# Decoder kernel on one core: attention outputs packed and divided by way of DMAs instead of transposes, scores in 64x64 array tiles, last keys in 32x32 tiles

## The chip, the cores and the metric

The kernel runs on one core of a Trainium2 chip. The metric is the device time of one execution in microseconds (us). Five engines work side by side and meet only at semaphores: PE (TensorE, matrix products into the eight PSUM banks), DVE (VectorE), ACT (ScalarE), POOL (GpSimd) and SP (SyncE, which here only issues DMAs). Each engine takes its instructions strictly in the order of the program.

## What is computed

Two decoder layers over x (4 batches, 512 positions, 128 features), float32, each sublayer followed by a residual sum and a layer norm:

```python
# layer 0: causal self attention, 16 heads of 8
scores = einsum('bshd,bthd->bhst', layernorm(q) / sqrt(8), layernorm(k)); softmax, causal
out = einsum('bhst,bthd->bshd', attn, v) @ W_out
# layer 0: cross attention, 16 heads of 8, 154 keys of the context
# layer 0: mixture of 8 experts (gates under 0.1 dropped)
# layer 1: linear attention (elu + 1), causal
# layer 1: cross attention, 8 heads of 128, 154 keys
# layer 1: gated feed-forward layer, 128 -> 384 -> 128
```

The change concerns the first two lines' attentions. A head has only 8 features, so neither the scores nor the weighted values fill the 128x128 array.

## The kernel before, in words

**Turns.** Self (a = 0) and cross (a = 1) attention of a batch b go by groups g of four heads: 32 turns (b, a, g), in the order of TURNS. The remaining sublayers of a batch ("rests", lines with x2T, gate, ex, lkq, XS, PT, XO, hid, down) are cut into small steps and laid between the turns. One list of steps, `schedule()`, is the program of all engines: every engine walks the whole list and issues what it has for each step. The order of that list is written out by hand as the string MERGE, the PSUM bank of each step as the digits of BANK_OF. Within the order an engine waits only for semaphores, and PE waits until a bank that it fills has been drained.

**A turn.** `scores` (S, L1117) computes scores with queries on partitions, for the maxima alone. Each "unit" fills a pair of banks, one for the upper 64 partitions of the packed queries and keys (r = 0), one for the lower (r = 1). A self unit is one or two pieces of causal length, and then four products with an identity that add the mask of the diagonal blocks (L1136). DVE takes the maxima from PSUM (`maxima`, L1832, L1837). `max_T` (mT, L1201) turns them into rows, ACT copies these, and SP places them by one DMA (L804) among the query rows, which `scores_T` (ST, L1158, mask L1165, last keys L1149) waits for: it computes the same scores with keys on partitions, the maxima already taken off. ACT writes their exponentials to EX (L1570). `values` (PV) multiplies with V (self, L1192) or with VX (cross, L1179), whose ninth column is 1, so each head yields 8 weighted values and the sum of its weights in its own 32 partitions. The 26 keys beyond 128 of the cross attention are one full product over all four heads, L1182, through the matrix VXR.

**From a turn to the output.** ACT copies the bank to `pvraw` (L1474). `products_T` (cT, L1204) transposes it in four pieces so that heads lie along the free axis, and DVE divides (`divided`, a reciprocal L1858 and a product L1860 into ctx). After the fourth turn `ctx_T` (L1209) transposes the four blocks of ctx back to features on partitions, ACT copies them to ctxT, and `out_product` (L1213, products L1220) multiplies with the output weights. The steps ctxT, out and norm of (b, a) are called a finish below; there are eight.

**Placements.** Queries and keys of a batch are split in three bf16 parts, and SP places them by 12 DMAs for self (L783) and 12 for cross attention (L797).

## Time and profile before

| | us |
|---|---|
| three runs | 486.65, 489.23, 489.41 (median 489.23) |
| the profiled execution, its time | 487.79 |
| its span from first to last instruction | 486.0 |
| PE busy | 459.1 (94%) |
| weight loads of PE busy | 304.6 (63%) |
| DVE busy | 378.0 (78%) |
| ACT busy | 344.3 (71%) |
| POOL busy | 187.5 (39%) |

The profiled execution took 1.8 us more than its span and lies 1.4 us below the median. A matrix product is pipelined: its recorded length has a tail that overlaps the next one, so what a group of products costs is read as the distance from its start to the start of the next group, not as its length. Products and weight loads of float32 are recorded twice each, transposes once.

### The profile page before, as it was taken

To read this page: it belongs to the slowest core of one execution; us is meant where nothing else is said; L and a number is where in the kernel's file an instruction comes from. 1 tells how busy PE (TensorE), PEld (TensorE's weight loads), DVE (VectorE), ACT (ScalarE), POOL (GpSimd) and SP (SyncE) were. 2 spreads that over 40 slices of the span, in tenths; PEclk is the share of its full clock that TensorE was granted. 3 is DMA by queue.
4 is the path that set the end of the run, shared out by engine and by line. 5 is a ranking of instruction groups with operands and counts; after the bars stand their busy time and mean duration, and the time that the engine had idled before them with its cause. 6 is when DMAs were issued, how large, how long until landed. Compare 5 with 4: busy or idle time off the path is not lost.

```text
span 486.0 us, 11581 instructions
## 1 busy us (share of the span) xinstructions
PE 459.1 (94%) x4048; PEld 304.6 (63%) x4048; DVE 378.0 (78%) x1083; ACT 344.3 (71%) x879; POOL 187.5 (39%) x349
## 2 busy tenths in 40 slices
PE   6687899999999999999999999999999999999995
PEld 4454557655455556666777565567764756896895
DVE  4489888798898999995798888847878678765557
ACT  3535758877868788877757787985776868958742
POOL 8590002650204452533233331433414536835423
PEclk9589999999999999999999999999999999999999
DMA  7851300033210211200003000030000000000001
GB/s 229 189 131 36 100 5 25 13 100 82 58 24 1 67 39 35 69 2 0 4 16 93 9 3 2 3 81 13 3 12 14 0 1 2 1 1 1 2 1 43
DMA packets 27181, 18.34 MB, mean 38 GB/s; under 512 B 8217, under 2 KB 26773, under 8 KB 26997
## 3 DMA queue, kind: packets, MB, share of 16 engines
q1 hardware_dynamic: 23413, 15.44, 12.0%
q10 hardware_dynamic: 3712, 2.17, 1.8%
q8 instruction: 33, 0.54, 0.5%
q14 instruction: 23, 0.19, 0.1%
HBM read 5.58 MB, written 1.05 MB: 14 GB/s over the span
## 4 chain that ended last, share of the span: by engine, by line
PE 38%; POOL 5%; DVE 4%; ACT 3%; issue 3%; SPq 1%; DMA 1%; POOLq 0%; DVEq 0%; ACTq 0%
PE psum L1066 5%; PE psum L1425 4%; PE psum L1436 4%; PE psum L1402 3%; PE psum L1338 3%; PE psum L1129 2%; PE psum L1158 2%; PE psum L1192 2%; PE psum L1182 2%; PE psum L1179 2%; SPq L797 1%; PE psum L1447 1%; POOL GP L1024 1%; POOL rstd_rest L955 1%; ACT REST L1653 1%
## 5 line engine op out<-in xcount | busy, mean ns | idle before, releaser
L1570 ACT ACTIVATE EX<-psum 128x1024 f32<-128x1024 f32 (+1 forms) x128 | 118.1, 979 | 12.9 <-PE psum L1165 8.3
L1837 DVE TENSOR_REDUCE mparts<-psum 128x2 f32<-128x768 f32 (+1 forms) x96 | 77.5, 861 | 4.8 <-PE psum L1136 4.5
L1832 DVE TENSOR_REDUCE mparts<-psum 128x4 f32<-128x616 f32 (+1 forms) x80 | 67.8, 875 | 4.7 <-PE psum L1129 4.0
L1129 PE MATMUL psum<-K,Q 64*128 64x154 bf16 (+4 forms) x512 | 47.4, 268 | 5.6 <-issue 2.1
L1024 POOL TENSOR_TENSOR GP<-REST,xrs 128x512 f32<-128x512 f32 (+1 forms) x48 | 33.1, 713 | 46.6 <-DVE xrs L2066 32.6
L1158 PE MATMUL psum<-Q,K 64*128 64x512 bf16 (+3 forms) x320 | 41.4, 315 | 3.6 <-DMA Q<-mrows 1.8
L1653 ACT ACTIVATE REST<-psum,nxmax 128x154 f32<-128x154 f32 x96 | 36.2, 396 | 10.1 <-DVE nxmax L2056 7.9
L1474 ACT COPY pvraw<-psum 128x512 f32<-128x512 f32 x32 | 18.7, 584 | 32.4 <-PE psum L1192 23.4
L1192 PE MATMUL psum<-EX,V 128*32 128x256 f32 (+3 forms) x512 | 37.7, 435 | 0.0
L1129 PEld LDWEIGHTS psum<-K,Q 64*128 64x128 bf16 x512 | 19.0, 95 | 28.9 <-issue 18.4
L952 POOL TENSOR_SCALAR rstd_rest<-moments_rest 128x2 f32<-128x2 f32 x32 | 7.3, 228 | 74.9 <-DVE moments_rest L1872 74.4
L952 POOL TENSOR_SCALAR rstd_attn<-moments_attn 128x4 f32<-128x4 f32 x8 | 1.9, 238 | 83.9 <-DVE moments_attn L1872 83.8
L2056 DVE TENSOR_REDUCE nxmax<-psum 128x2 f32<-128x308 f32 x64 | 28.8, 469 | 5.6 <-PE psum L1402 5.2
L1402 PE MATMUL psum<-GP,xT 128*128 128x308 f32 x96 | 30.5, 433 | 0.1
L1192 PEld LDWEIGHTS psum<-EX,V 128*32 128x32 f32 x512 | 14.6, 109 | 18.4 <-issue 16.9
L1136 PE MATMUL psum<-maskS,ident 64*128 64x128 bf16 (+2 forms) x320 | 24.7, 232 | 0.0
L1698 ACT ACTIVATE X<-Y_rest,shift_rest,rstd_rest 128x128 f32<-128x128 f32 x36 | 15.9, 493 | 11.8 <-POOL shift_rest L960 11.7
L1425 PE MATMUL psum<-VM,REST 128*128 128x128 f32 x192 | 23.8, 277 | 0.2 <-DVE VX L1928 0.2
L955 POOL TENSOR_TENSOR rstd_rest<-rstd_rest,power 128x2 f32<-128x2 f32 x32 | 22.9, 716 | 2.7
L1165 PE MATMUL psum<-maskT,ident 64*128 64x128 bf16 (+2 forms) x320 | 23.8, 227 | 0.0
L1425 PEld LDWEIGHTS psum<-VM,REST 128*128 128x128 f32 x192 | 22.6, 192 | 1.3 <-issue 0.7
L1158 PEld LDWEIGHTS psum<-Q,K 64*128 64x128 bf16 x320 | 13.0, 94 | 15.9 <-issue 6.8
(343 smaller groups left out, 1150.2 us busy)
## 6 DMA issues: line engine op xcount, KB each, us to landing
Q<-xparts SPq DMA_DIRECT2D x24, 128.0 KB
Q<-parts SPq DMA_DIRECT2D x21, 128.0 KB
K<-parts SPq DMA_DIRECT2D x21, 128.0 KB
X<-in_x SPq DMA_DIRECT2D x4, 256.0 KB, 3.1
Q<-in_L_xattn_Wkv SPq DMA_DIRECT2D x1, 1024.0 KB, 7.2
K<-xkparts SPq DMA_DIRECT2D x24, 38.5 KB
out<-XB_rest SPq DMA_DIRECT2D x6, 128.0 KB, 1.8
Q<-in_L_xattn_Wq SPq DMA_DIRECT2D x1, 512.0 KB, 4.3
```

What stands on the lines that cost most here:

```text
L955: return nc.gpsimd.tensor_tensor(to, to, half_power, ALU.pow)
L1024: last = nc.gpsimd.tensor_tensor(of.XP[:, at:at + 4 * n].rearrange("p (h c) -> p h c", h=4)[:, :, 0:c1 - c0], of.XE[:, :, c0:c1], of.xrs.r ...
L1129: last = mm(to[:, r, at:at + n], Q6[a][p, b % 2, 2 * g + jj, P * q:P * q + P], K6[a][p, b % 2, 2 * g + jj, 0:n], start=at == 0 or bool(a), ...
L1158: last = mm(to[:, r, at:at + n], K6[a][p, b % 2, 2 * g + jj, P * k:P * k + P], Q6[a][p, b % 2, 2 * g + jj, P * k:S], start=at == 0 or bool ...
L1192: last = mm(to[32 * h:32 * h + 32, P * k:S], V[:, k, 4 * g + h, :], EX[:, ex_slot(b, a, g, u) + h % 2, at:at + n], start=k == PV_ORDER[0], ...
L1402: fills_(mm(fill(key)[:, 0:2 * C], half_of(b, h).xT[4][:, P * q:P * q + P], G[:, head:head + 2, :].rearrange("p h c -> p (h c)")), key)
L1425: mm(to, of.XPT[:, head, :], VM[:, head, :], start=head == 0, stop=False)
L1570: drains(nc.scalar.activation(dst, src, ACT.Exp), key)
L1653: last = nc.scalar.activation(of.XE[:, i, :], src[:, C * j:C * j + C], ACT.Exp, bias=of.nxmax[:, i:i + 1], accum_out=of.xsum[:, i:i + 1])
L1832: last = vec.tensor_reduce(nmax[:, :, :, q], src[:, :, 0:2 * n].rearrange("p r (j k) -> p r j k", j=2), AX.X, ALU.max, negate=True)
L1837: last = vec.tensor_reduce(nmax[:, :, jj, q], src[:, :, at:at + P * (q + 1)], AX.X, ALU.max, negate=True)
L2056: vec.tensor_reduce(of.nxmax[:, 2 * side:2 * side + 2], src, AX.X, ALU.max, negate=True).then_inc(xmax_ready[z], 1)
```

## The change

1. The weights of the values are laid out so that the 8 weighted values of a head fall on partitions 0, 4, ..., 28 of its 32 and the sum on partition 1. After ACT's copy to pvraw, two DMAs on SP's queue (`pack`) put the values of the turn on 32 neighbouring partitions of `weighed[a]` and the four rows of sums, cut in eighths, on 32 partitions of `sums_of[a]`. The four transposes of `products_T` and DVE's two operations per turn are gone.
2. Once per finish DVE inverts the sums in place (128x64, `invert`), one DMA writes them to DRAM (`keep_inverses`), another reads them back with each head's row repeated on 8 partitions into ctxT (`spread_inverses`, step "fan"), and DVE multiplies (`divide`, 128x512). The transposes of `ctx_T` and ACT's copy are gone.
3. Scores: where a product had 64 rows and 128 columns of the array, there are now two of 64x64 (`in_tiles`), four tiles in all. In self attention each half of the queries or keys takes only its causal length; the masks go by the same tiles.
4. Cross values: a pair of banks holds the two halves of the queries. The last keys are eight products of 32x32 tiles with 256 columns (`rests`), in place of one 128x128 product of 512 columns; the scores of these keys are laid out to match.
5. MERGE and BANK_OF are written anew for the new steps. A memset of POOL is cut in eight.

```diff
 def finish_steps(b, a):
+    yield b, "invert", a
+    yield b, "fan", a
     yield b, "ctxT", a
     yield b, "out", a
     yield b, "norm", a
...
+            def pack(b, a, g):
+
+                drained(sp, (b, "PV", a, g))
+                if b or g:
+                    sp.wait_ge(packed[a], 32 * (NQ * b + g))
+                if b and g == 0:
+                    sp.wait_ge(divided[a], b)
+                at = slice(32 * g, 32 * g + 32)
+                sp.dma_start(sums_of[a][at, :], pvraw[1:P:32, :]).then_inc(packed[a], 16)
+                sp.dma_start(weighed[a][at, :], pvraw[0:P:4, :]).then_inc(packed[a], 16)
+
+            def keep_inverses(b, a):
+
+                i = finishes.index((b, a))
+                sp.wait_ge(inverted, i + 1)
+                if i:
+                    sp.wait_ge(inverses_spread, 16 * i)
+                sp.dma_start(inverses.rearrange("h (c t) -> (h c) t", c=HD), sums_of[a][:, :]
+                             ).then_inc(inverses_kept, 16)
+
+            def spread_inverses(b, a):
+
+                i = finishes.index((b, a))
+                sp.wait_ge(inverses_kept, 16 * (i + 1))
+                if i:
+                    b0, a0 = finishes[i - 1]
+                    filled(sp, (b0, "out", a0))
+                sp.dma_start(ctxT[:, :], inverses.rearrange("h (o t) -> h o t", o=1).to_broadcast(
+                    [H, HD, S])).then_inc(inverses_spread, 16)
...
+            def in_tiles():
+
+                for e in R:
+                    for r in R:
+                        yield e, r, *[slice(TILE * i, TILE * i + TILE) for i in (e, r)]
...
                 for at, jj, q in PIECES[a][u]:
-                    n = C if a else P * (q + 1)
-                    for r in R:
-                        p = slice(TILE * r, TILE * r + TILE)
-                        last = mm(to[:, r, at:at + n], Q6[a][p, b % 2, 2 * g + jj, P * q:P * q + P],
-                                  K6[a][p, b % 2, 2 * g + jj, 0:n], start=at == 0 or bool(a), stop=bool(a))
+                    for e, r, half, p in in_tiles():
+
+                        n = C if a else P * q + TILE * (e + 1)
+                        last = mm(to[half, r, at:at + n],
+                                  Q6[a][p, b % 2, 2 * g + jj, P * q + TILE * e:P * q + TILE * e + TILE],
+                                  K6[a][p, b % 2, 2 * g + jj, 0:n], start=bool(a) or at == 0,
+                                  stop=bool(a), skip_group_check=not a)
...
+                    to = pair(key)
+                    for n in HALVES:
+                        for h in range(4):
+                            mm(to[32 * h:32 * h + 32, n, 0:HS], VX[:, 4 * g + h, :],
+                               EX[:, ex_slot(b, a, g, h // 2) + h % 2, HS * n:HS * n + HS],
+                               start=True, stop=False, skip_group_check=True)
+                    for n, h, rest, cols in rests():
+                        last = mm(to[32 * h:32 * h + 32, n, 0:HS], VXR[rest, 4 * g + h, :],
+                                  EX[rest, ex_slot(b, a, g, 2), cols], start=False, stop=True,
+                                  skip_group_check=True)
...
-            def products_T(b, a, g):
-                drained(pe, (b, "PV", a, g))
-                transposes((b, "cT", a, g), [(P * n, pvraw[:, P * n:P * n + P])
-                                             for n in range(NB)])
-
-            def ctx_T(b, a):
-                drained(pe, (b, "cT", a, NQ - 1))
-                to_features((b, "ctxT", a), ctx[a][:, :, :, :].rearrange("p n h d -> p n (h d)"))
-
             def out_product(b, a):
-                drained(pe, (b, "ctxT", a))
+                pe.wait_ge(divided[a], b + 1)
...
+            def products_out(b, a, g):
+                key = (b, "PV", a, g)
+                filled(act, key)
+                if TURN[b, a, g]:
+
+                    b0, a0, g0 = TURNS[TURN[b, a, g] - 1]
+                    act.wait_ge(packed[a0], 32 * (NQ * b0 + g0 + 1))
...
+            def invert(b, a):
+
+                dve.wait_ge(packed[a], 32 * NQ * (b + 1))
+                vec.reciprocal(sums_of[a][:, :], sums_of[a][:, :]).then_inc(inverted, 1)
+
+            def divide(b, a):
+
+                dve.wait_ge(inverses_spread, 16 * (finishes.index((b, a)) + 1))
+                vec.tensor_tensor(ctxT[:, :], weighed[a][:, :], ctxT[:, :], ALU.mult
+                                  ).then_inc(divided[a], 1)
```

One line of the table of the order, before and now (the last turn and finish of batch 3 lie near its end):

```diff
-    "1101pp0p00kf1kkf101100k10fk0112k2122310032310031022210023001100113321100321110113200"
+    "pptttk11p0pxp1pf01k11f1k0010kkfkkf1011001f100112312230213102002130223100311002013010"
```

**Place 1: PE, two units of self scores.** Before: a unit of keys times queries for two pieces of one head pair (384 and 128 columns) with its masks, and the start of one with a single piece of 512.

```order
L1129 MATMUL psum<-K_0,Q_0 128x384 x2
L1129 MATMUL psum<-K_0,Q_0 128x128 x2
L1136 MATMUL psum<-maskS,ident 128x2x64 x2
L1136 MATMUL psum<-maskS,ident 128x256 x2
L1158 MATMUL psum<-Q_0,K_0 128x512 x2
L1165 MATMUL psum<-maskT,ident 128x64 x2
L1165 MATMUL psum<-maskT,ident 128x128 x2
```

Now, the same kinds of unit (the two stand in another stretch):

```order
L1217 MATMUL psum<-Q_0,K_0 64x512 x2
L1217 MATMUL psum<-Q_0,K_0 64x448 x2
L1172 MATMUL psum<-maskT,ident 64x64 x2
L1172 MATMUL psum<-maskT,ident 64x128 x2
...
L1190 MATMUL psum<-K_0,Q_0 64x320 x2
L1190 MATMUL psum<-K_0,Q_0 64x384 x2
L1190 MATMUL psum<-K_0,Q_0 64x64 x2
L1190 MATMUL psum<-K_0,Q_0 64x128 x2
L1172 MATMUL psum<-maskS,ident 64x256 x2
L1172 MATMUL psum<-maskS,ident 64x2x64 x2
```

A unit with one piece went from 6 to 8 products, one with two pieces from 8 to 12; each product writes 64 partitions instead of 128.

**Place 2: PE, the finish of batch 3's self attention** (L1220 before and L1279 now are its output product; K_1 and Q_1 belong to cross attention). Before:

```order
L1129 MATMUL psum<-K_1,Q_1 128x154 x8
L1066 MATMUL psum<-ident,ctx_self 128x128 x4
L1353 MATMUL psum<-lwv,xT 128x128 x2
L1129 MATMUL psum<-K_1,Q_1 128x154 x8
L1179 MATMUL psum<-EX,VX 32x512 x4
L1182 MATMUL psum<-EX,VXR 128x512
L1220 MATMUL psum<-wout,ctxT 128x128 x4
```

Now:

```order
L1190 MATMUL psum<-K_1,Q_1 64x154 x8
L1111 MATMUL psum<-ident,X 128x128 x2
L1217 MATMUL psum<-Q_1,K_1 64x512 x8
L1244 MATMUL psum<-EX,VX 32x256 x8
L1248 MATMUL psum<-EX,VXR 32x256 x8
L1269 MATMUL psum<-identb,mparts 80x128
L1111 MATMUL psum<-ident,REST 128x128 x2
L1461 MATMUL psum<-GP,xT 128x308
L1190 MATMUL psum<-K_1,Q_1 64x154 x8
L1279 MATMUL psum<-wout,ctxT 128x128 x4
```

The transposes of ctx are gone, the last keys are eight small products, and a cross unit has 8 score products (a row of x8 was two units before and is one now). From the last self values of batch 3 to this output product the list has 34 steps, where it had 22.

**Place 3: DVE, the last finish** (batch 3, cross attention; what waits for packed1 and inverses_spread waits for DMAs). Before:

```order
L1872 BN_AGGR moments_rest<-stats_rest 128x2
L1858 RECIPROCAL rsum<-psum 128x16 [waits bank_filled0,bank_drained0]
L1860 TENSOR_TENSOR ctx_cross<-psum,rsum 128x4x32 [waits dve_step]
L2005 TENSOR_TENSOR vaug<-psum,rows 128x2x128 [waits bank_filled3]
L1998 TENSOR_TENSOR REST<-REST 128x512 [waits phi_exps0]
L1883 TENSOR_TENSOR Y_attn<-psum,XB_attn 128x512 [waits residual_ready,x_ready2,bank_filled1]
```

Now:

```order
L2031 TENSOR_TENSOR gl<-gl,gs 128x16 [waits dve_step]
L1924 RECIPROCAL sums_cross<-sums_cross 128x64 [waits packed1]
L2039 TENSOR_TENSOR Y_rest<-psum,X 128x256 [waits rest_x_ready1,bank_filled2]
L2053 SCALAR_TENSOR_TENSOR Y_rest<-psum,gl,Y_rest 128x128 [waits bank_filled0,bank_drained2,gates_ready1]
...
L2063 TENSOR_TENSOR REST<-REST 128x512 [waits phi_exps0]
L1929 TENSOR_TENSOR ctxT<-weighed_cross,ctxT 128x512 [waits inverses_spread]
L1950 TENSOR_TENSOR Y_attn<-psum,XB_attn 128x512 [waits residual_ready,x_ready2,bank_filled7]
```

The reciprocal moved from behind a PSUM bank to behind two DMAs, with the expert sums (L2053) queued behind it, and the product that makes ctxT stands behind two DMAs more.

## Rows read from the trace of the kernel before

**Rows 1.** Page: busy time, and three rows of the 40 slices.
```profile
PE 459.1 (94%) x4048; PEld 304.6 (63%) x4048; DVE 378.0 (78%) x1083; ACT 344.3 (71%) x879; POOL 187.5 (39%) x349
...
PE   6687899999999999999999999999999999999995
...
DVE  4489888798898999995798888847878678765557
```
**Rows 2.** Busy us by stretch; then PEclk, DMA share, GB/s.
```profile
27.00:391.00 364.00, 354.99 (x3424) 222.59 (x3425) 303.99 (x807) 270.85 (x618) 123.54 (x227) 1.00 0.13 33
391.00:486.00 95.00, 87.93 (x575) 71.03 (x573) 61.78 (x225) 62.90 (x242) 44.91 (x86) 0.99 0.02 7
90.00:210.00 120.00, 117.85 (x1185) 67.25 (x1184) 108.70 (x292) 94.09 (x189) 45.90 (x74) 1.00 0.19 49
```
**Rows 3.** Timeline of PE from 228 us: start, length, engine, line.
```profile
228.78 0.60 PE L1066 MATMUL psum<-ident,pvraw 128*128 128x128 f32 x4
229.21 0.22 PE L1201 MATMUL psum<-identb,mparts 128*80 128x128 bf16 x1
```
**Rows 4.** Timeline of PE from 222 us: the values of a cross turn.
```profile
222.30 1.07 PE L1179 MATMUL psum<-EX,VX 128*32 128x512 f32 x8
223.30 1.12 PE L1182 MATMUL psum<-EX,VXR 128*128 128x512 f32 x2
224.26 0.93 PE L1066 MATMUL psum<-ident,GP 128*128 128x128 f32 x7
```
**Rows 5.** Timeline of PE from 64 us: self units following each other.
```profile
64.24 0.39 PE L1129 MATMUL psum<-K,Q 64*128 64x384 bf16 x4
...
64.63 0.38 PE L1158 MATMUL psum<-Q,K 64*128 64x512 bf16 x2
64.85 0.25 PE L1165 MATMUL psum<-maskT,ident 64*128 64x64 bf16 x4
64.93 0.38 PE L1129 MATMUL psum<-K,Q 64*128 64x384 bf16 x4
```
**Rows 6.** Timeline of PE from 319 us: scores of the last keys.
```profile
319.58 0.40 PE L1149 MATMUL psum<-Q,K 64*32 64x512 bf16 x4
319.96 1.27 PE L1402 MATMUL psum<-GP,xT 128*128 128x308 f32 x4
```
**Rows 7.** Timeline of all engines at 310 us: two cross units.
```profile
310.02 0.44 PE L1129 MATMUL psum<-K,Q 64*128 64x154 bf16 x8
...
310.39 0.77 PE L1066 MATMUL psum<-ident,GP 128*128 128x128 f32 x5
```
**Rows 8.** Weight loads by form: busy us, mean ns | idle us before.
```profile
L1129 PEld LDWEIGHTS psum<-K,Q 64*128 64x128 bf16 x512 | 19.0, 95 | 28.9 <-issue 18.4 <-ACT EX L1570 2.9 <-DMA Q<-xparts 1.7
...
L1201 PEld LDWEIGHTS psum<-identb,mparts 128*80 128x80 bf16 x32 | 3.7, 117 | 2.4 <-issue 2.0
```
**Rows 9.** DVE by form, same columns.
```profile
L1858 DVE RECIPROCAL rsum<-psum 128x16 f32<-128x16 f32 x32 | 8.0, 249 | 3.8 <-PE psum L1066 3.6
...
L1860 DVE TENSOR_TENSOR ctx_self<-psum,rsum 128x128 f32<-128x128 f32 x16 | 4.7, 292 | 0.5
...
L1998 DVE TENSOR_TENSOR REST<-REST 128x512 f32<-128x512 f32 x6 | 4.2, 697 | 2.4 <-ACT REST L1640 2.4
```
**Rows 10.** Longest of SP's own waits: total us, times, longest.
```profile
SPq L445 <- ACT mrows L1579: 199.6, 30, 13.9
```
**Rows 11.** The DMA of the maxima: ns min/median/max; who waited for it, us, times.
```profile
L804 SPq DMA_DIRECT2D Q<-mrows x32: 707/765/852, 35.9 to 369.2; - x32
...
  PE psum L1158: 1.8, 2
```
**Rows 12.** Chain of waits: the flight of the last DMA of a placement.
```profile
326.68 2.46 DMA Q<-xparts
```
**Rows 13.** Timeline of all engines at the last finish.
```profile
380.50 0.58 ACT L1474 COPY pvraw<-psum 128x512 f32<-128x512 f32 x1 [0.87 <-PE psum L1182]
...
384.44 1.16 PE L1220 MATMUL psum<-xwo,ctxT 128*128 128x128 f32 x8
```

More of the change, by code:

```diff
@@ L257, in takes @@
         return [(b, "PV", *at)]
-    if what == "cT":
-        return [(b, "PV_out", *at)]
+    if what == "pack":
+        return [(b, "PV_out", *at)] + ([(b - 1, "ctxT", at[0])] if b else [])
+    if what == "invert":
+        return [(b, "pack", at[0], NQ - 1)]
+    if what == "fan":
+        return [(b, "invert", at[0])]
     if what == "ctxT":
-        return [(b, "cT", at[0], NQ - 1)]
+        return [(b, "fan", at[0])]
     if what == "out":
@@ L328, in in_pair @@
 def in_pair(step):
-    return step[1] in ("S", "ST") and not (step[1] == "ST" and step[2] and step[4] == 2)
+    _, what, *at = step
+    return (what == "S" or what == "ST" and not (at[0] and at[2] == 2)
+            or what == "PV" and at[0] == 1)
 STREAMS = "stpfrlwcvxu0123k"
 MERGE = (
-    "rrrrrrrrlwrrlllwrrrurrsssssuuuvuuuuussssstttrsrttslssspptssttttpsslsrppsttststtupllu"
-    "sssppststtsttpuussssppttpsufswttfuusstsusssfwpptursxffttsurrrrrctstspcfccppttpstsrrw"
-    "kttkssrpspllttssttptssssslppsstpsskfsttftsstppstsflwsppssptsktsrtssfpfctppsstcstpssp"
@@ L495, in build @@
         causal = sb("causal", [P, P], BF16)
[L497 removed]
+        ident2 = sb("ident2", [P, TILE], BF16)
         maskS = sb("maskS", [P, 2, P], BF16)
@@ L1004, in wM @@
                     pool.wait_ge(bank_filled[k], m + 1)
-                    nc.gpsimd.memset(words(Q6[1].rearrange("p b h t -> p (b h) t")), 0.0
-                                     ).then_inc(cross_rows_ready, 1)
+                    zeroed = words(Q6[1].rearrange("p b h t -> p (b h) t"))
+                    for i in range(8):
+                        last = nc.gpsimd.memset(zeroed[:, S * i:S * i + S], 0.0)
+                    last.then_inc(cross_rows_ready, 1)
                     step(nc.gpsimd.memset(XP, 0.0))
@@ L1125, in scores @@
                 for at, jj, q in PIECES[a][u]:
[L1126 to L1138 removed]
+                    for e, r, half, p in in_tiles():
+                        n = C if a else P * q + TILE * (e + 1)
[3 more added lines that the diff above has]
+                                  stop=bool(a), skip_group_check=not a)
+                if not a:
+                    last = mask(to, [at + P * q for at, _, q in PIECES[0][u]], maskS,
+                                [slice(0, P), slice(TILE, P)])
                 fills_(last, key)
@@ L1579, in max_T @@
                 drains(copy(mrows[:, parity(b, a, g), :], src[0:48, 0:64].bitcast(BF16)), key)
+            def products_out(b, a, g):
[4 more added lines that the diff above has]
+                    act.wait_ge(packed[a0], 32 * (NQ * b0 + g0 + 1))
+                drains(copy(halved(pvraw[:, :]), pair(key)[:, :, 0:HS]) if a else
+                       copy(pvraw[:, :], bank(key)), key)
             def setup_T(b, n):
```

160 lines of the change are left out of this document (76 added, 84 removed).

## Prediction, written before the changed kernel ran

> **What bounds the kernel now.** I read the page's busy times first [rows 1]: PE is busy 94% of the span, DVE 78%, ACT 71%. In the 40 slices PE stands at 9 from the sixth slice to the last but one, so it is PE everywhere except at the start; DVE, though, stands at 8 or 9 through most of the first half. A busy PE is not yet a bound, because its ends are modelled, so I looked at a stretch. From 27 us (the first scores) to 391 us (the last finish) PE is busy 355.0 of 364 us and DVE 304.0, at a granted clock of 1.00, that is 2.4 GHz [rows 2]. And the groups on PE follow each other at the pace of their columns: in rows 5 a self unit of two pieces (512 columns, masks 384 more) takes 0.39 us from start to start and one of one piece (512 and 192) takes 0.30 us; 896 and 704 columns at 2.4 GHz would be 0.37 and 0.29. So PE streams columns with no slack, and what the change takes from the column counts comes off the time, until something else is late. From 391 us on there are only rests, which the change doesn't touch: 95 us that stay.
>
> **Part 1, the transposes.** The four transposes of pvraw take 0.43 us from start to start [rows 3], not the 0.60 of their record. 32 turns: 13.8 us. The transposes of ctx are the same form, 8 finishes: 3.4 us. Together 17.2 us off PE. (ACT loses 8 copies of 0.6 us; it isn't late anywhere, so I count nothing.)
>
> **Part 2, the last keys.** L1182 takes 0.96 us from start to start, as one product of 512 columns over the whole array; L1179 beside it does four products of 512 columns, each in 32 columns of the array, in 1.00 [rows 4]. So column tiles run side by side. Tiles that differ in rows and columns at once: the nearest are [rows 6], four products of 512 columns, 64 rows by 32 columns, in 0.38 us from start to start, the switch of tiles included; one after another they would be 2048 columns, 0.85 us at 2.4 GHz. Now: eight 32x32 products of 256 columns. All side by side they cost half of L1179, 0.50 us; if the two halves follow each other, 1.00. I take 0.50, since the eight tiles are all different: 16 turns x 0.46 = 7.4 us gained, and at the other end a loss of 0.6. L1179 itself, cut in two halves of 256 columns, keeps its column count, and I leave it at 1.00.
>
> **Part 3, self scores.** With 64x64 tiles the tile e = 0 of a one-piece unit streams 448 columns and a mask of 128, e = 1 streams 512 and 64: 576 each instead of 704. A two-piece unit comes to 640 on every tile instead of 896. At the pace of rows 5 (0.43 ns a column) that is 0.245 and 0.275 us for 0.30 and 0.39. A turn has two and three of them for scores and the same again for transposed scores: 2 x 0.055 + 3 x 0.115 = 0.455 us, x 2 x 16 turns = 14.6 us. Cross scores keep their columns (154 and 512).
>
> **Part 4, more instructions.** Self turns have 32 more products each, cross turns 24 more for scores and 11 for values: some 1070 more pairs of weight load and product. Does PE keep up? The densest in the trace are the four masks from 64.85 to 64.93, 20 ns each [rows 5]. A two-piece unit now wants 12 in 0.275 us, 23 ns each: just possible. Two cross units (8 products) take 0.37 us now, their entry included [rows 7]; 16 products at 20 ns are 0.32, so they just fit. If the pace is 31 ns (what a one-piece unit now needs, 0.245 / 8, and no row shows less for long), the 96 two-piece units lose 0.10 us each and the 32 pairs of cross units 0.13: 13.8 us. The other end is 0. I take 3 us, near the 20 ns row.
>
> On the weight loads themselves: a bf16 load of 128 columns takes 95 ns and one of only 80 columns takes 117 [rows 8], so narrower isn't quicker. The Trainium skill says the same from the other side: in TensorEngine Tiling (Array Packing), Restrictions, column tiling switches the fast weight load off, and in TensorE: Matmul & The Clock Gate, Packing small matmuls, loads overlap products only where the row group differs; its section on LDWEIGHTS gives a load as columns / 1.2 ns, an estimate of 53 ns for 64 columns, six in a row for a row group of a two-piece unit = 0.32 us against 0.275. The trace agrees that the narrow load is slower, and no row shows whether two such loads in one row group queue up.
>
> PE in sum: -17.2 - 7.4 - 14.6 + 3 = **-36.2 us**.
>
> **Part 5, what is late next.** DVE loses 32 x (0.249 + 0.292) = 17.3 us and gains 8 x (0.70 for a 128x512 product, 0.25 for the reciprocal) = 7.6 [rows 9]. In the stretch of 364 us it goes to 294.3, PE to 355.0 - 36.2 = 318.8. But from 90 to 210 us, some 11 turns, PE has 117.9 and DVE 108.7 [rows 2]; minus 11/32 of each change they stand at 105.4 and 105.4. Two engines in strict order that depend on each other aren't both busy 98% of the time, as PE is today; at 95% the stretch takes 111 us, so 9 of 12.4 us arrive. I put +4 us for this and the like stretch around 30 to 60 us.
>
> **Part 6, the waits that are added.** From ACT's copy to the output product the last finish takes 3.94 us today [rows 13]. Now: copy 0.6, two issues of 0.77 [rows 11], a flight of 2.46 [rows 12], reciprocal 0.25, then twice issue and flight (3.2 each), product 0.70: 12.0 us. Of the DRAM end no row says more than this; if it lands later, each finish grows by that. The list leaves 26 to 45 steps between the last values and the output product of a finish, where it left 12 to 34; at the average of 0.46 us a step (486 us, 1047 steps) the shortest gap is 12 us, just what the chain needs. So PE hardly waits; but DVE does. Its reciprocal stands one to five instructions behind the values, can start only 4.6 us after them, and the maxima or expert sums of the next steps are queued behind it (place 3 in the change); PE then waits for the banks that these would drain. I estimate 2 us at each reciprocal and 1 at each product for ctxT, 24 us of DVE waiting in all. DVE has 364 - 36 - 294 = 34 us free in the stretch, so I charge a third: +8 us, bounds 0 and 24. The last finish has no attention behind it to hide in: +1 us.
>
> SP gets 64 + 16 DMAs at 0.77 = 62 us of issuing. It waits 199.6 us for the rows of maxima alone [rows 10], so the time is there; the order is another matter (rival C).
>
> **Sum**: 487.8 (the profiled execution) - 36.2 + 4 + 8 + 1 = **464.6 us**. That execution lies 1.4 us under the median of the runs, which I ignore. I say 465.
>
> The Trainium skill has a rule on the flight: DMA: Bandwidth & Descriptors, section Anatomy of one DMA, puts about 2.0 us of fixed cost on every transfer, most of it the receipt of the write, and HBM is its heaviest target. The trace agrees in size: 2.46 us for a placement from SBUF to SBUF [rows 12]. With 2.0 for it three flights would be 1.4 us shorter per finish; with a dearer write to DRAM they would be longer, and no row here has such a write with somebody waiting.
>
> **Rivals.**
> A. *The small tiles don't reach their pace.* For it: the 80-column load of 117 ns [rows 8], and that no row shows more than four products in a row at 20 ns. Against: the first two or four products of a self unit are long, so the short ones can be prepared meanwhile. Part 4 then costs 13.8 instead of 3, part 2 gains nothing (8.0 lost): 464.6 + 10.8 + 8.0 = 483. The Trainium skill's rule on loads, as told in part 4, ends here too.
> B. *PE stays the only bound.* For it: DVE has 34 us of room, and eight banks let PE run ahead of a waiting DVE. Against: DVE at 9 in the early slices. No terms of parts 5 and 6: 487.8 - 36.2 = 452.
> C. *SP's queue makes the maxima late; slower.* Place: the DMA of the maxima (mT), for which the transposed scores of each turn wait. `pack` now stands before it in the same queue, waits for ACT's copy of the values of another turn, and issues two DMAs, 1.5 us; ahead of four of them also stands the wait for a reciprocal and for a write to DRAM. Against: today PE waits for this DMA only twice, 1.8 us [rows 11], and 30 times SP waits for the row, not the row for SP [rows 10]. It decides from 36 / 32 = 1.1 us a turn. At 1.5 us, the two issues, plus another 0.3 of waiting, it is 32 x 1.8 = 58 us - 36 = +22, so 510; with half of the turns hit, 481. The place it would start from is 1.1 us x 32.
> D. *The change gives little because DVE's waits aren't hidden*: 24 us instead of 8, and half of rival A: 464.6 + 16 + 9 = 490.
>
> **Chances.** Forecast 0.62, A 0.10, B 0.12, C 0.08, D 0.08. A measurement of this kernel can tell about 1% from no change, that is 484.3 and 494.1. Forecast and B are faster (0.74); A ends at 483 and is split, 0.05 and 0.05 within 1%; D is within 1% for three quarters, C slower. So faster 0.79, within 1% 0.11, slower 0.10. The range goes from 450 (B's 452, less 2 for shorter gaps between groups than I count) to 488, which takes in A and nearly half of D.
>
> **What would show it.** Right: in the profile after, a two-piece self unit at 0.27 to 0.29 us from start to start and the last keys at 0.5 to 0.6; PE's busy time near 425 with its share a little under 94%; waits of DVE on DMAs (reciprocal, product for ctxT) of 1 to 3 us each, sixteen of them; the stretch after the last finish at 95 us as before. Wrong: units at 0.37 or more (A); PE waiting on the DMA of the maxima for tens of us (C); DVE waits over 20 us in sum with PE waiting for banks behind them (D), or none, with a span near 450 (B).

## The result, and the profile after

The changed kernel takes 492.33 us (median of 6 runs, 490.12 to 494.68), the kernel before 487.93 (6 runs): ratio 1.0086, 95% interval 1.0059 to 1.0113. Forecast were 465, range 450 to 488. The prediction was wrong, in size and in sign. Runs over 1.5% above the fastest of their kernel are left out of every median and ratio here (two of the four of h2, one each of i2 and k3).

The page after, busy times and the slices of PE, DVE and PEclk:

```profile
PE 439.6 (90%) x5136; PEld 286.6 (59%) x5136; DVE 375.5 (77%) x1035; ACT 343.2 (70%) x871; POOL 190.3 (39%) x356
...
PE   7668798878898899899999999999999989999994
...
DVE  4489878797889889988599878857985678764556
...
PEclk9598999998999899999999999999999999999998
```

Against [rows 1], PE has 19.5 us less to do (459.1 to 439.6) in a span that is 3.4 us longer (489.4 for 486.0). So PE's idle time went from 26.9 to 49.8 us. DVE is nearly where it was (378.0).

Stretches after (busy us of PE, PEld, DVE, ACT, POOL, then PEclk, DMA share, GB/s):

```profile
27.00:391.00 364.00, 331.00 (x4493) 199.96 (x4494) 299.66 (x761) 265.49 (x601) 123.46 (x228) 0.98 0.18 47
391.00:489.40 98.40, 89.92 (x580) 73.53 (x579) 64.56 (x235) 65.34 (x245) 47.73 (x93) 0.99 0.02 7
90.00:210.00 120.00, 105.06 (x1564) 57.52 (x1559) 105.03 (x264) 87.98 (x167) 39.73 (x68) 0.97 0.22 57
30.00:90.00 60.00, 49.21 (x877) 28.69 (x868) 50.28 (x85) 36.90 (x55) 14.93 (x25) 0.94 0.22 60
```

In the same 30 to 90 us the kernel before had:

```profile
30.00:90.00 60.00, 54.89 (x726) 34.70 (x723) 52.62 (x102) 41.19 (x66) 10.31 (x17) 0.99 0.15 41
```

The removed products left holes, and in the stretches with holes the granted clock is lower: 0.94 for 0.99, and 0.97 for 1.00 from 90 to 210 us [rows 2]. The last output product of the attentions starts at 388.8 us instead of 385.3, and the time from there to the end is the same in both, 101 us. So the loss arises in the attentions. It doesn't grow evenly: the row of maxima of the 14th turn (L1201 before, L1269 now) is transposed at 152.2 us instead of 143.0, that of the last turn at 368.6 instead of 367.4. As steps have changed places between such marks, they show where time passes and not what costs it.

PE after, from 45 us, self units; and from 125 us, a cross turn:

```profile
46.94 0.40 PE L1217 MATMUL psum<-Q,K 64*64 64x512 bf16 x4 [0.15 <-ACT pvraw L1651]
47.15 0.23 PE L1172 MATMUL psum<-maskT,ident 64*64 64x64 bf16 x4
47.18 0.36 PE L1190 MATMUL psum<-K,Q 64*64 64x320 bf16 x5
...
125.20 0.33 PE L1190 MATMUL psum<-K,Q 64*64 64x154 bf16 x8 [0.58 <-DVE mparts L1903]
125.36 0.39 PE L1217 MATMUL psum<-Q,K 64*64 64x512 bf16 x4
...
125.81 1.07 PE L1244 MATMUL psum<-EX,VX 128*32 128x256 f32 x16
126.81 0.66 PE L1248 MATMUL psum<-EX,VXR 32*32 32x256 f32 x16
127.40 0.33 PE L1190 MATMUL psum<-K,Q 64*64 64x154 bf16 x8
```

The first shows a one-piece self unit in 0.24 us (46.94 to 47.18), where [rows 5] had 0.30. Over all the units that are followed by one of their own tile shape, the median start to start is 0.27 us for one piece (35 units, before 0.31) and 0.30 for two (37 units, before 0.39). The cross unit of eight products takes 0.16 us, the last keys 0.59 (before 0.96), L1244 keeps 1.00. The operations are as fast as forecast.

The chain of waits after, followed back over nearly the whole span, shares of the span:

```profile
PE 56%; DVE 17%; ACT 11%; POOL 7%; issue 5%; SPq 2%; DMA 1%; POOLq 0%; ACTq 0%; DVEq 0%
```

PE has 56 of its 99 points. The chain of the kernel before can be followed back to 215 us only; again as shares of the whole span, and one of its pieces:

```profile
PE 38%; POOL 5%; DVE 4%; ACT 3%; issue 3%; SPq 1%; DMA 1%; POOLq 0%; DVEq 0%; ACTq 0%
```
```profile
223.37 1.05 PE psum L1182 x2
```

There PE has 38 of 55 points, and of the ten pairs of the last keys (L1182) in its reach eight are on it. So PE's work was on the path that decided the end. The chain doesn't say how close behind it the next path lies; the experiments do.

The longest waits of PE and of DVE after (total us, times, longest):

```profile
PE psum L1269 <- DVE mparts L1918: 5.9, 6, 1.8
...
PE psum L1190 <- DVE mparts L1903: 2.3, 4, 0.8
PE psum L1190 <- ACT EX L1632: 2.0, 3, 0.8
PE psum L1217 <- DVE mparts L1908: 1.8, 5, 0.5
```
```profile
DVE mparts L1908 <- PE psum L1172: 12.0, 13, 2.1
...
DVE sums_cross L1924 <- DMA weighed_cross<-pvraw: 3.1, 1, 3.1
```

PE waits for DVE's maxima, and DVE waits for PE's scores (12.0 us). No wait is long, and PE waits directly for none of the new DMAs; DVE waits for them 3.5 us in all (3.1 here, 0.4 for the inverses), and PE with its weight loads 1.6 us for DVE's product behind them.

The last finish after:

```profile
377.30 0.59 ACT L1650 COPY pvraw<-psum 128x512 f32<-128x512 f32 x1
...
378.50 0.51 SPq L828 DMA_DIRECT2D weighed_cross<-pvraw  x1
380.53 0.55 DVE L1924 RECIPROCAL sums_cross<-sums_cross 128x64 f32<-128x64 f32 x1 [3.10 <-DMA weighed_cross<-pvraw]
381.11 0.34 SPq L836 DMA_DIRECT2D inverses<-sums_cross  x1
382.61 0.58 SPq L846 DMA_DIRECT2D ctxT<-inverses  x1
387.03 0.68 DVE L1929 TENSOR_TENSOR ctxT<-weighed_cross,ctxT 128x512 f32<-128x512 f32 x1
387.94 1.16 PE L1279 MATMUL psum<-xwo,ctxT 128*128 128x128 f32 x8
```

From the copy to the output product 10.6 us, forecast 12.0, before 3.9 [rows 13]. The reciprocal takes 0.55 us, not the forecast 0.25.

DVE has only 2.5 us less to do than before, where the forecast took off 9.7. One term was overlooked: the matrix for the last keys is four times as wide, and DVE writes it 16 times.

```profile
L1923 DVE TENSOR_TENSOR VXR<-psum,rows x16: 169/186/196, 33.9 to 337.0; 26x32 f32<-26x32 f32 x16
```
```profile
L1990 DVE TENSOR_TENSOR VXR<-psum,rows x16: 313/390/409, 69.3 to 344.5; 26x128 f32<-26x128 f32 x16
```

The first is the kernel before, the second the changed one (ns: least, median, most): some 3 us more.

### The profile page after: what moved, and what is told of

It is laid out like the page before. It is cut to its first block, busy times and chain, and to the rows that moved or that the text cites. A ratio compares the mean times of both kernels' runs of the same rounds, so it can differ in the third digit from the quotient of the medians.

```text
span 489.4 us, 13835 instructions
## 1 busy us (share of the span) xinstructions
PE 439.6 (90%) x5136; PEld 286.6 (59%) x5136; DVE 375.5 (77%) x1035; ACT 343.2 (70%) x871; POOL 190.3 (39%) x356
## 4 chain that ended last, share of the span: by engine, by line
PE 56%; DVE 17%; ACT 11%; POOL 7%; issue 5%; SPq 2%; DMA 1%; POOLq 0%; ACTq 0%; DVEq 0%
PE psum L1111 6%; PE psum L1484 6%; PE psum L1260 5%; PE psum L1397 5%; PE psum L1461 5%; DVE mparts L1908 5%; PE psum L1190 4%; ACT EX L1632 3%; DVE mparts L1903 3%; PE psum L1217 3%; PE psum L1495 2%; PE psum L1244 2%; PE psum L1353 1%; PE psum L1486 1%; PE psum L1146 1%
## 5 line engine op out<-in xcount | busy, mean ns | idle before, releaser
L1190 PE MATMUL psum<-K,Q 64*64 64x154 bf16 (+8 forms) x1024 | 50.6, 273 | 8.8 <-DVE mparts L1903 2.3
L1217 PE MATMUL psum<-Q,K 64*64 64x512 bf16 (+7 forms) x640 | 43.2, 316 | 6.8 <-DVE mparts L1908 1.8
L1725 ACT ACTIVATE REST<-psum,nxmax 128x154 f32<-128x154 f32 x96 | 36.2, 395 | 10.5 <-DVE nxmax L2121 10.3
L1190 PEld LDWEIGHTS psum<-K,Q 64*64 64x64 bf16 x1024 | 22.8, 108 | 34.0 <-issue 16.7
L1260 PE MATMUL psum<-EX,V 128*32 128x256 f32 (+3 forms) x512 | 40.5, 458 | 1.3 <-DVE mparts L1908 1.1
L995 POOL TENSOR_SCALAR rstd_rest<-moments_rest 128x2 f32<-128x2 f32 x32 | 7.7, 239 | 72.0 <-DVE moments_rest L1939 71.8
L1217 PEld LDWEIGHTS psum<-Q,K 64*64 64x64 bf16 x640 | 15.6, 105 | 26.9 <-issue 10.0
L1651 ACT COPY pvraw<-psum 128x512 f32<-128x512 f32 x16 | 9.4, 585 | 29.4 <-PE psum L1260 29.4
L1111 PE MATMUL psum<-ident,X 128*128 128x128 f32 x90 | 18.1, 302 | 5.8 <-ACT X L1758 1.0
L1397 PE MATMUL psum<-ew,xT 128*128 128x512 f32 x48 | 22.9, 610 | 0.0
L1172 PE MATMUL psum<-maskS,ident 64*64 64x128 bf16 (+2 forms) x320 | 21.8, 236 | 0.0
```

Of the source, the lines that this page charges most:

```text
L1111: last = nc.tensor.transpose(to[0:n, at:at + m], src, ident[0:m, 0:m])
L1190: last = mm(to[half, r, at:at + n], Q6[a][p, b % 2, 2 * g + jj, P * q + TILE * e:P * q + TILE * e + TILE], K6[a][p, b % 2, 2 * g + jj, 0:n ...
L1217: last = mm(to[half, r, at + q - P * k:at + S - P * k], K6[a][p, b % 2, 2 * g + jj, P * k + TILE * e:P * k + TILE * e + TILE], Q6[a][p, b ...
L1260: last = mm(to[32 * h:32 * h + 32, P * k:S], V[:, k, 4 * g + h, :], EX[:, ex_slot(b, a, g, u) + h % 2, at:at + n], start=k == PV_ORDER[0], ...
L1397: fills_(mm(fill(key), half_of(b, h).xT[2][:, P * i:P * i + P], ew[:, 4 * side:4 * side + 4, :].rearrange("p e d -> p (e d)")), key)
L1725: last = nc.scalar.activation(of.XE[:, i, :], src[:, C * j:C * j + C], ACT.Exp, bias=of.nxmax[:, i:i + 1], accum_out=of.xsum[:, i:i + 1])
```

## The experiments

All ratios are against the kernel before in the same job, whose medians were 486.9 to 488.2 us. The names in brackets (e1, g2 and so on) are used again further down.

**What is a microsecond of PE worth?** The 64x64 tiles alone, put into the kernel before (the code is that of the change, parts 3):

> The kernel before with part 3 of the change alone: scores, transposed scores and their masks in 64x64 tiles, order and banks as before. Theory S (the small tiles cost what they save in columns, because each weight load and product has a pace of its own): no gain, 486 to 494 us. Theory O (the tiles gain their columns, and the new order or the DMA path gave it back): 487.9 less 11 to 14, so 474 to 477. Theory W (before wasn't bound by PE alone, so that PE's time off turns into waiting for DVE and ACT): 480 to 485, with PE's busy share down.

Measured (e1) 485.77 us, ratio 0.9973 (0.9942 to 1.0005): not clear of no change, and far from theory O. The last keys left out of the kernel before (their 26 keys are missing from the values):

```diff
-                    fills_(mm(to, VXR[:, g, :], EX[:, ex_slot(b, a, g, 2), :], start=False, stop=True,
+                    fills_(mm(to[0:32, 0:8], VX[:, 4 * g, :], EX[:, ex_slot(b, a, g, 2), 0:8],
```

> The kernel before without the 16 products of the last keys (L1182, 0.96 us each, 15.4 us of PE); left out: the 26 last keys' part of the cross attention. It measures what a microsecond taken off PE alone is worth in the old order. If PE is the only bound, as I predicted: 472 to 474 us. Theory W: 478 to 484, the rest as idle time of PE.

Measured (e3) 485.48 us, 0.9943 (0.9914 to 0.9971). The page:

```profile
PE 447.8 (92%) x4048; PEld 303.2 (63%) x4048; DVE 377.4 (78%) x1083; ACT 343.7 (71%) x879; POOL 187.3 (39%) x349
```

16 products of 0.96 us gone, 15.4 us, and 2.3 us came back (487.7 to 485.5). The engine that was 94% busy simply idles more. Both times lie just above the ranges of theory W. The transposes, the division and the copy of ctxT left out of the kernel before (nothing is divided, ctxT is constant):

```diff
-            work = {..., "mT": max_T, "cT": products_T, "ctxT": ctx_T, "out": out_product,
+            work = {..., "mT": max_T, "out": out_product,
```

> The kernel before without the transposes of pvraw and of ctx, without DVE's division and ACT's copy to ctxT, and with nothing in their place (the output product reads a constant); left out: division and regrouping of the heads. It is the bound of what parts 1 and 2 of the change can give in the old order: 17.2 us off PE, 17.3 off DVE. If PE bounds: 470 to 472. If DVE bounds the self turns as well: below 470, since both fall. If it stays over 478, the order itself (banks, chains between engines) holds the time, and theory W stands.

Measured (e4) 484.23 us, 0.9924 (0.9899 to 0.9949): 16.7 us less of PE and 14.5 of DVE for 3.5 us. All three together, and that with DVE relieved by maxima over half of the columns:

```diff
-                        last = vec.tensor_reduce(nmax[:, :, jj, q], src[:, :, at:at + P * (q + 1)],
+                        last = vec.tensor_reduce(nmax[:, :, jj, q], src[:, :, at:at + TILE * (q + 1)],
```

> The kernel before with three reliefs of PE together: 64x64 score tiles, no product of the last keys, no transposes of the weighted values and no division (17 us off DVE too). PE's busy time falls by some 40 us. Alone they gave 2.0, 2.8 and 3.5 us. V: PE has long stopped being the bound, the sum is no more than 6 to 9 us, 478 to 482. P: the reliefs must add up once all of them are in, 450 to 460. C: 475 to 480.

> Both at once: 40 us off PE and 80 us off DVE. V: no better than the half maxima alone by more than 10 us. P: as the three PE reliefs alone. C: the two together give far more than the sum of what each gives alone: with 8 for the one and 5 for the other, over 30 us, 440 to 457.

> The kernel before, with DVE's maxima taken over half of the columns (the maxima are then of a part of the keys only); some 65 us off DVE's 378, nothing off PE's 459. Theory V (once PE is relieved a little, and already before, DVE is what the attentions go by): the time falls by 25 us or more, 450 to 463. Theory P (PE after all): no change, 485 to 489. Theory C (PE and DVE both run in strict order through the same banks and hand each other their delays; neither is the bound alone): a few us, 478 to 484.

Measured: PE's reliefs together (g2) 479.91 us, 0.9827 (0.9779 to 0.9876); with half maxima too (g3) 476.71, 0.9743 (0.9678 to 0.9807); half maxima alone (g1) 486.10, 0.9953 (0.9925 to 0.9980). The page of the one with both:

```profile
PE 423.8 (89%) x4720; PEld 284.5 (60%) x4720; DVE 306.2 (64%) x1020; ACT 338.3 (71%) x871; POOL 186.4 (39%) x349
```

35.3 us off PE and 71.8 off DVE give 11.4. Theory P (PE bounds) falls with g2, V (DVE bounds) with g1, where 57 us off DVE gave 2.1, and the strong form of C with g3: within the noise the effects add (8.2 and 2.1 against 11.4), they don't multiply.

**Is it ACT, or the one turn that EX holds?** Exponentials over half of the columns, then half of the products of the self values left out:

```diff
+                    if TURN[b, a, g]:
+                        dst, src = EX[:, slot_:slot_ + 2, 0:HS], pair(key)[:, :, 0:HS]
```

> The kernel before with the three reliefs of PE (479.9 us), and ACT's exponentials over half of the columns (the rest of EX keeps older values). Theory E: the attentions go round a loop between ACT and PE, since EX holds one turn: five exponentials (4.9 us) of a self turn, then its values (2.36 us), in which ACT can write no exponential, then the copy to pvraw (0.6 us), then the next exponentials; 8 us a turn whatever else is saved. Half exponentials take 2.2 us out of a self turn's loop and 0.9 out of a cross turn's, 50 us in all, until PE's 424 us bound it: 445 to 458. Theory C (strict order, delays handed on everywhere, no loop in particular): 474 to 479, as the half maxima gave 3.

> The kernel before with half exponentials alone. E: the loop becomes shorter than PE's own work, and PE (459 us busy) takes over: 472 to 480. Theory P: no change. C: 483 to 487.

> The same with half of the products of the self values left out (8 of 16 a turn, 1.2 us of 2.36). It is PE time like that of the other reliefs, of which 40 us gave 8, but it lies in the loop of theory E: 16 turns x 1.1 to 1.2 = 18 us, 461 to 467. Theory C: 3 us or less, 476 to 480.

Measured: 474.12 us for the first (h1; 0.9719, 0.9683 to 0.9755), 5.8 below its base of 479.9, where the loop wanted 22 or more; half exponentials alone (h0) 486.20 (0.9966, 0.9939 to 0.9994), with ACT at 304.3 us for 344.3. Half values (h2) 476.55 (0.9767, 0.9687 to 0.9847) from two runs, 3.4 below their base, where the loop wanted 13 or more. All four runs lie far apart and follow the clock: 472.2 us of span at 0.973, 477.5 at 0.966, 479.5 and 479.7 at 0.955. Theory E as one loop that sets the turn is refuted by h1; h2 agrees, but two runs are a weak test. Then the order itself, by hand: the first unit of the next turn's transposed scores ahead of the values, and ACT waiting for the products that read its slots alone:

```diff
-                if first >= 0 and (first == 0 or EX_USER[first] != EX_USER[first - 2]):
-                    filled(act, (EX_USER[first][0], "PV", *EX_USER[first][1:]))
+                if first >= 0 and first in SLOT_READ:
+                    act.wait_ge(slots_free, SLOT_READ[first])
...
+                    if k in (0, 3):
+                        last.then_inc(slots_free, 1)
```

> A whole kernel: before, with the 64x64 score tiles, ACT waiting for the products that read its slots of EX and not for all of the values, and in 22 turns the first unit of the next turn's transposed scores issued ahead of the values. E: the first exponential of a turn no longer waits for the end of the values, for the copy and for its own scores, about 1 us less in each of these turns: 485.8 (tiles alone) - 15 to 20 = 466 to 471. C: 482 to 487.

Measured (i2) 541.94 us, 1.1105 (1.1061 to 1.1149). The largest effect of the study, in the wrong direction. Its longest waits of PE, the longest of ACT (L1221 are the values of a self turn), and the stretch of the attentions:

```profile
PE psum L1188 <- DMA Q<-mrows: 19.9, 11, 2.3
PE psum L1188 <- DVE mparts L1869: 9.8, 9, 3.2
PE psum L1188 <- DVE mparts L1864: 8.0, 4, 3.9
```
```profile
ACT EX L1602 <- PE psum L1221: 42.3, 14, 7.4
```
```profile
27.00:440.00 413.00, 360.88 (x4226) 218.94 (x4227) 298.49 (x790) 270.85 (x609) 119.55 (x220) 0.95 0.12 30
```

The transposed scores, put ahead, wait for the row of maxima (in the kernel before 1.8 us in all [rows 11]), and the values, whose exponentials have been ready, are queued behind them. ACT, which had no such wait among its longest before, waits 42.3 us for those values. I read this as two tight loops, exponentials to values and scores to maxima to transposed scores, of which the move helps the one and hurts the other. The release and the new order were made together, and neither was run alone, so which of them costs how much isn't shown.

**Is the packing to blame, and what does DVE count for now?** The changed kernel without the packing's 80 DMAs, the reciprocals and the products for ctxT (nothing is divided), and the changed kernel with half maxima:

```diff
-            work = {..., "mT": mT, "pack": pack, "invert": keep_inverses, "fan": spread_inverses, ...
+            work = {..., "mT": mT, ...
```

> The changed kernel without its 80 DMAs, the reciprocal and the product for ctxT (the output product reads a constant); left out: division and regrouping. Order, banks and tiles as changed. Theory D (the waits on the DMAs and SP's queue gave the gain back): 465 to 478. Theory O, with the order and the banks at fault, or S: 486 to 491, since only 3.5 us of DVE's waits in the trace are for these DMAs.

> The changed kernel with maxima over half of the columns. Its PE is already relieved by 20 us. V: the 36 us that the forecast took off PE come through now, 450 to 462. C: 460 to 475, more than the kernel before gains from the same edit. P or the queue of DMAs as bound: no change, 489 to 493.

Measured: without packing (e5) 488.37 us, 1.0000 (0.9965 to 1.0035); with half maxima (g4) 484.93, 0.9937 (0.9915 to 0.9960). The path by DMAs, with DVE's work for it, costs 4.0 us (492.3 to 488.4; the two intervals leave 2 to 6). The steps between hide the DMAs of a finish: without a single one, e5 still takes 10.6 us from the last copy to the output product.

```profile
374.89 0.58 ACT L1645 COPY pvraw<-psum 128x512 f32<-128x512 f32 x1
...
385.53 1.16 PE L1278 MATMUL psum<-xwo,ctxT 128*128 128x128 f32 x8
```

And the same relief of DVE that gave 2.1 us in the kernel before gives 7.4 in the changed one. DVE has become dearer, in the direction of part 5, though g4 came out above the ranges of V and C. (g4's clock is also higher than the changed kernel's, 0.978 for 0.968; the section on the clock has what that may be worth.)

**Is it the order?** MERGE and BANK_OF alone were rewritten by a search that moves single steps and replays each order with the durations of the profile; one line of the table of the first:

```diff
-    "sssppststtsttpuussssppttpsufswttfuusstsusssfwpptursxffttsurrrrrctstspcfccppttpstsrrw"
+    "ssspputsttststpuuwssssppttpstsfuftsustsufssppstrufwrfusrstrrcttrpcstfspptrsttsrcpcwt"
```

> The kernel before, its instructions unchanged, MERGE and BANK_OF alone written anew. The order was found by moving single steps, each order replayed with the durations of the profile of before (each instruction's own length, products by their columns, the waits of the program) and kept when it ended earlier. Theory O (what bounds all these kernels is the order: four engines hand each other short waits, and a microsecond saved anywhere is lost at the next wait): the same work in a better order gains more than all the reliefs of PE and DVE did, some 12 to 15 us, 471 to 477. Theory C' (the order is already as good as the work allows): 484 to 490, or slower, as the hand-made move of the transposed scores was.

> The kernel before with the 64x64 score tiles, order and banks found in the same way with its own instructions. O, with PE not the bound: within 1 us of the reordered kernel before, though PE has 15 us less to do. Theory P' (once the order is right, PE is the bound as the prediction had it): 8 us or more below it.

> The changed kernel with order and banks found in the same way. If its own order was what lost the gain, it now comes out below the reordered kernel before, 455 to 468. If the change itself brings nothing, since it takes from PE what PE has to spare and adds a chain of DMAs: level with the other two or up to 3 us above them, 472 to 478.

Measured: 504.93 us (j1; 1.0364, 1.0330 to 1.0398), 498.59 (j2; 1.0232, 1.0200 to 1.0265), 504.23 (j3; 1.0333, 1.0293 to 1.0373). All three slower than the hand-made orders. Between themselves they say something too: in its searched order the kernel with 64x64 tiles is 6.3 us faster than the kernel before in its own, where in the old order the tiles gave 2.0. Unless j2's order just happens to be the better one, the price of PE's time depends on the order. And j3 is level with j1. The search had used what the replay left out; looking for it in the traces gave the change of tile shape. Two self units of one piece of the kernel before, followed by their own shape and by whole-array transposes:

```profile
37.95 0.39 PE L1158 MATMUL psum<-Q,K 64*128 64x512 bf16 x2 [1.09 <-DMA Q<-mrows]
...
38.26 0.38 PE L1158 MATMUL psum<-Q,K 64*128 64x512 bf16 x2
...
51.15 0.39 PE L1129 MATMUL psum<-K,Q 64*128 64x512 bf16 x2
...
51.55 0.66 PE L1066 MATMUL psum<-ident,qkn 128*128 128x128 f32 x4
```

0.31 us to the next start in the one case, 0.40 in the other; over all such units the medians are 0.312 (43 followed by their own shape) and 0.395 (21 by another). It isn't the longer float32 load of what follows: before the bf16 products of 64x32 tiles (L1149) it is 0.39 in the one case that there is. Changing the tile shape costs PE some 0.08 us. PE changes it 330 times in the kernel before, 362 in the changed one and 388 in j1; 58 times 0.08 is an estimated 5 us of PE, so this is at most a part of j1's 17. (The Trainium skill has the mechanism, without a figure: TensorEngine Tiling (Array Packing), Tiling Modes, Key Properties, says that a change of the tiling mode drains the engine. The rows fit this.) A second search knew this, though with 0.1 to 0.15 us a change, and the load behind a wait:

> The kernel before with a second order of its own, found like the first but with two costs that the first search did not know and that the traces show: about 0.1 to 0.15 us each time PE goes from one tile shape to another, and the weight load of 0.1 to 0.2 us behind a wait of PE. With them the replay gives back all 17 profiled spans, from 472 to 541 us, within 6 us, the two bad orders included. Theory O: 474 to 480. If it is again over 490, the search finds only what the replay leaves out, and nothing follows on how good the order of before is.

> The changed kernel in a second order, found in the same way. If the change is worth nothing in any order: level with the reordered kernel before, 474 to 480. If the change frees something that its own order did not use: 3 us or more below it. If its chain of DMAs costs in any order: 2 to 4 us above it.

Measured 490.56 us (k1; 1.0063, 1.0035 to 1.0091) and 492.85 (k3; 1.0076, 1.0034 to 1.0118; its runs go from 488.0 to 494.5). Better than the first search by 14 and 11 us, no better than the orders in the files. By the bound written down beforehand for k1, theory O isn't shown: whether a clearly better order exists stays open. What is shown is that the same instructions in another order cost 17 us more (487.5 to 504.9), more than any relief gave back.

The last one, both reliefs that leave the result whole:

> The kernel before with the 64x64 score tiles and with maxima over half of the columns: each key or query half is left out of the search for the shift, which the division takes out again, so the result is that of the reference up to rounding as long as no exponential overflows. Alone the tiles gave 2.0 us (0.9973) and the half maxima 2.1 us (0.9953). Theory C (no engine is the bound, each gives back a tenth to a fifth of what is taken off it): the two add up to 4 to 6 us, 481.5 to 484. A bound that both reach together would show as 475 or less.

Measured (l1) 485.50 us, 0.9968 (0.9944 to 0.9992), a smaller gain than either theory expected. Two gains of 2 us, each with an interval of some 1.3 us to either side, can't show whether they add up. The fastest kernel of the study with a whole result is the changed one with half maxima (g4), 0.6% below the one before.

## The clock

Every run lists its span and mean granted clock. The changed kernel's six: 0.980 and 488.4 us, 0.969 and 489.4, 0.969 and 489.7, 0.966 and 491.5, 0.963 and 491.7, 0.962 and 492.9. One program, and its time follows its clock. The slope of these six is 2.4 us per 0.01, of the ten runs of e5 3.1, of the nine of k3 3.2; over the 132 runs of the changed kernel and all experiments, each taken against its own kernel's mean, 2.9 us per 0.01 (correlation -0.70). The medians are 0.984 for the kernel before, 0.978 without packing, 0.968 for the changed one. Less work on PE doesn't always lower it: e3 and e4 kept 0.983 and 0.984.

The size fits: 0.01 of 489 us is 9.8 us at 1.2 GHz instead of 2.4, in which PE does half its work, so 4.9 us if all that time were PE's. From 0.984 to 0.968 it is 3.8 to 4.6 us at 2.4 to 2.9 per 0.01, against a loss of 4.4. By this estimate the changed kernel at the clock of the one before would be about level with it, and some 3 of the 4.0 us of the packing, and of the 7.4 of g4, are clock too. It is a correlation within kernels, carried over to a difference between two; what comes first, waits of PE or clock, it doesn't say. A kernel that fills PE's holes with idle products would tell, and wasn't tried.

## Why the prediction was wrong, point by point

- **The bound: the step that failed.** "PE streams columns with no slack, and what the change takes from the column counts comes off the time." It took 94% busy, a digit 9 and two units at the pace of their columns as a bound, and counted every microsecond off PE as one off the time. PE was on the deciding path, but other paths lay just behind it, and the "something else" that the forecast priced at 4 and 8 us took nearly all. Taken off PE alone, 15.4 us gave 2.3 (e3), and the tiles, 14.6 us by the forecast and 9.3 of busy time, gave 2.0 (e1); everything together, 35.8 us of PE's busy time and 16.1 of DVE's, gave 8.2 (g2). In the order of before a microsecond on PE was worth some 0.15 to 0.25 us, not 1. Nor was there "no slack": of the 42 one-piece units at a granted clock of 1.00 that their own tile shape follows, 11 take over 0.36 us for 0.31, and of the 58 with two pieces 14 take over 0.44 for 0.39. The tails of the records can hide such time, as here (0.55 us from start to start, no idle time in the view):

```profile
48.26 0.39 PE L1158 MATMUL psum<-Q,K 64*128 64x128 bf16 x4
48.49 0.33 PE L1165 MATMUL psum<-maskT,ident 64*128 64x128 bf16 x4
48.81 0.39 PE L1158 MATMUL psum<-Q,K 64*128 64x128 bf16 x4
```

(The Trainium skill warns of the reading: Perfetto Trace Analysis, at its head, calls the busy time of the matmul row a bad metric for how close a kernel is to its roofline, because matmuls are pipelined. One of the two it names instead, the weight load's share, stood at 63% [rows 1].)
- **Parts 1 to 4, PE's sum of -36.2.** Operations right: units 0.27 and 0.30 us, at best 0.24 and 0.27 (forecast 0.245 and 0.275; from 0.31 and 0.39), last keys 0.59 (0.50), L1244 unchanged, cross units fit. Rival A is refuted by these rows. Busy time fell by 19.5 and not by some 34, to 439.6, not 425. The last keys and units came out a tenth over; records at half clock, which are longer (0.62 us for the 0.40 of the same score product), may be another part, and the tails of the additional products a third. These weren't separated.
- **Part 5, DVE next: +4.** The direction was right: half maxima give 7.4 us in the changed kernel, 2.1 in the one before. But DVE is not the next bound: 58 us off it (375.5 to 317.3) gave those 7.4. No run prices the term itself. Its working left out that VXR became wider (3 us), and the reciprocals took 0.55 us for 0.25.
- **Part 6, added waits: +8, +1.** Forecast were 24 us of DVE waiting on DMAs, measured 3.5; the finish grew to 10.6 us (12.0), and e5 shows that the steps between hide its DMAs. The price of the whole path, 4.0 us in e5, is half of the 8. The write to DRAM landed in 1.5 us in the middle, so it wasn't the dearer one that the prediction feared; the read from it, 3.4, was dearer than the 2.46 that was taken for it.
- **Rivals.** B (452) falls with the first point. C: no product waits for the DMA of the maxima, and PE's weight loads do so for 2.0 us in all, four times; SP waits for the rows, not they for SP. D ended nearest (490) by luck, since the waits on DMAs, its reason, are small. None said that the gain would be lost because other paths end just behind PE's; that case was missing.
- **Sum.** The measured steps, each with its place: the reliefs of PE in the order of before -8.2 (g2, 479.9 us). The changed kernel without packing has the same reliefs, except that the last keys still take 16 x 0.59 us of PE, which at the prices above is 1 to 2 us; it takes 488.4 (e5). The remaining 7 us are a difference and not a measurement: the new order with its banks, the values of a cross turn in a pair of banks, the wider VXR, and 53 more changes of tile shape than g2 (362 for 309) are all in it. These weren't separated, and a lower clock isn't the reason (0.978 in e5, 0.974 in g2). The packing adds 4.0. So what the changed kernel lost beyond the missing gain is open for its larger part.

## What to carry to other kernels

A busy share near 100% on one of several engines that run in strict order and hand work back and forth is no proof of a bound: take one operation of the busiest engine out and time that before pricing a change by it; here a microsecond of PE was worth 0.15 to 0.25, and it may be another in another order. The chain of waits doesn't give the price either: PE had 38 of its 55 points before, and L1182 was on it, for 2.3 us of 15.4. Holes in PE may be paid for twice: from 90 to 210 us the granted clock was 0.97 for 1.00 where PE was busy 105 us for 118.

## What was not expected of the hardware

- A change of tile shape on PE costs about 0.08 us (0.31 to 0.40 us for the same unit), from 64x64 tiles about 0.10 (0.27 to 0.37).
- Twelve pairs of load and product of 64x64 tiles run in 0.30 us, 25 ns a pair; eight 32x32 float32 products of 256 columns in 0.59, 1.2 times an ideal half of L1179's 1.00.
- The time of one and the same program follows its mean granted clock by some 2.4 to 3.2 us per 0.01.
- SP issues the new DMAs in 0.34 to 0.59 us (medians), not the 0.77 of the row of maxima; the small write to DRAM lands in 1.5 us (once 3.1), the spread read from it in 3.4 (3.1 to 3.8).
